# The minimum of a unit's scores, moved from behind the next unit's first eviction to in front of it

## What is computed

```python
q = _fq_sym(q, axis=-1)
k = _fq_sym(k, axis=-1)
v = _fq_sym(v, axis=2)
attn = jnp.einsum('bhqd,bhkd->bhqk', q, k)
attn = jax.nn.softmax(attn.astype(jnp.float32), axis=-1)
attn = _fq_unsigned(attn, axis=-1)
out = jnp.einsum('bhqk,bhkd->bhqd', attn, v)
```

## Time and profile before

| | us |
|---|---|
| median of three runs | 6005.62 (5996.2 to 6013.94) |
| the profiled execution, its own time | 5989.42 |
| its span (first to last instruction) | 5987.6 |
| VectorE busy in the span | 5458.4 (91%) |
| ScalarE busy | 4786.4 (80%) |
| GpSimd busy | 4741.8 (79%) |
| TensorE matmul busy | 4167.8 (70%) |
| first and last eviction of the cross attention (L918) start at | 344.9 and 5165.7 |

### The profile page before, as it was taken

The page is one execution under the profiler, slowest core; times in us unless marked ns, Lnnn a source line. Parts: engine busy times, 40 slices in busy tenths (PEclk is TensorE's granted clock), DMA queues, the critical chain, the costliest instruction groups (busy, mean ns, idle before and its releaser), DMA issues. The chain is left out here.

```text
span 5987.6 us, 141205 instructions
## 1 busy us (share of the span) xinstructions
PE 4167.8 (70%) x48324; PEld 2004.7 (33%) x49040; DVE 5458.4 (91%) x7655; ACT 4786.4 (80%) x6737; POOL 4741.8 (79%) x3414
## 2 busy tenths in 40 slices
PE   7656666666666666666666666666666666579898
PEld 3422222222222222222222222222222222346665
DVE  8889999999999999999999999999999999665444
ACT  5459999999899989989998899989999999646321
POOL 4558888888888888888888898888888888545351
PEclk9889999999999999999999999999999999889899
DMA  4167777777777777777777777777777777530243
GB/s 127 58 130 142 141 141 145 142 142 139 141 143 141 140 142 142 142 139 144 143 142 137 157 143 142 141 140 142 142 141 145 142 141 141 123 73 0 63 148 104
DMA packets 2282498, 783.42 MB, mean 131 GB/s; under 512 B 2189505, under 2 KB 2255908, under 8 KB 2276071
## 3 DMA queue, kind: packets, MB, share of 16 engines
q1 hardware_dynamic: 2239943, 604.79, 49.0%
q0 software_dynamic: 42272, 175.98, 15.6%
HBM read 187.41 MB, written 56.17 MB: 41 GB/s over the span
## 5 line engine op out<-in xcount | busy, mean ns | idle before, releaser
L918 DVE TENSOR_SCALAR_CACHE_REDUCE scores<-ring,step 128x2048 f32<-128x2048 f32 (+2 forms) x2560 | 4780.7, 1918 | 47.6 <-PE ring L845 35.5
L977 ACT ACTIVATE n_op<-scores,bias 128x2048 uint8<-128x2048 f32 x2048 | 4076.0, 1997 | 289.9 <-DVE m_rest L925 289.8
L793 POOL CAST nT<-pairs 128x2048 f16<-128x2048 uint8 x2048 | 3795.7, 1893 | 506.4 <-DMA pairs<-n_op 488.7
L845 PE MATMUL ring<-x_all,q_op 128*128 128x512 bf16 x7746 | 2149.8, 385 | 703.9 <-DVE scores L918 631.1
L845 PEld LDWEIGHTS ring<-x_all,q_op 128*128 128x128 bf16 x8192 | 683.2, 98 | 1856.2 <-DVE scores L918 1181.0
L842 PE MATMUL ring<-x_all,q_op 128*128 128x512 bf16 x1793 | 572.1, 389 | 778.6 <-DVE scores L918 747.6
L857 PE MATMUL pO<-nT,v_op 128*32 128x128 f16 x32768 | 659.7, 223 | 135.4 <-ACT att_g L995 109.4
L857 PEld LDWEIGHTS pO<-nT,v_op 128*32 128x32 f16 x32768 | 482.2, 98 | 585.1 <-issue 514.7
L842 PEld LDWEIGHTS ring<-x_all,q_op 128*128 128x128 bf16 x2048 | 116.8, 97 | 1001.6 <-DVE scores L918 983.6
L977 ACT ACTIVATION_READ_ACCUMULATOR n_op<-scores,bias 128x1 f32 x2048 | 395.1, 193 | 0.0
L1001 ACT COPY oT<-pO 128x512 f32<-128x512 f32 x128 | 75.0, 586 | 218.6 <-PE pO L857 218.6
(11 more groups left out here) (233 smaller groups left out, 3416.5 us busy)
## 6 DMA issues: line engine op xcount, KB each, us to landing
x_all<-keys_transposed POOLq DMA_DIRECT2D x128, 768.0 KB, 8.7
v_st<-value_integers POOLq DMA_DIRECT2D x128, 256.0 KB, 3.5
pairs<-n_op SPq DMA_TRANSPOSE x2048, 2.7
keys_transposed<-kT_s POOLq DMA_DIRECT2D x32, 384.0 KB, 3.3
xs<-expert_slots_in SPq DMA_DIRECT2D x78, 128.5 KB, 2.1
expert_slots_in<-zero_row SPq DMA_DIRECT2D x6, 1664.0 KB, 17.8
cT<-in_ctx_T SPq DMA_DIRECT2D x32, 256.0 KB, 2.6
z_all<-expert_outputs SPq DMA_DIRECT2D x4, 2048.0 KB, 11.7
```

The lines of the kernel that those rows point to most:

```text
L793: nc.gpsimd.tensor_copy(nT[par][:, j * EK:(j + 1) * EK, :].rearrange("p (a c) b -> p a c b", c=2), src).then_inc(s_un, 1)
L845: mm = nc.tensor.matmul(slot(t, j)[:, n * BANK:(n + 1) * BANK], q_op[b][:, t * P:(t + 1) * P], k_op[b][:, at + n * BANK:at + (n + 1) * BAN ...
L918: nc.vector.tensor_scalar(score[t % 2][:, at:at + width * BANK], slot(t, j)[:, 0:width * BANK], step[b][:, t:t + 1], None, ALU.mult, ALU.m ...
L977: nc.scalar.activation(n_op[par][:, j * EW:(j + 1) * EW], score[par][:, j * EW:(j + 1) * EW], ACT.Exp, bias=bias[par][:], scale=-1.0, accu ...
```

## The change

The two first entries of VectorE's list of steps change places.

```diff
-        DVE_STEPS = "D0 BIAS D1 D2 D3 INV D4".split()
+        DVE_STEPS = "BIAS D0 D1 D2 D3 INV D4".split()
```

## The result

| | before | after |
|---|---|---|
| time, median of 4 runs | 6000.91 us (5988.19 to 6013.94) | 6239.31 us (6237.09 to 6266.34) |
| profiled execution, own time | 5989.42 us | 6266.34 us |
| its span, mean granted clock of TensorE | 5987.6 us, 0.970 | 6263.8 us, 0.934 |

The change makes the kernel slower: 1.0407 times the time before, 95% interval 1.037 to 1.0445. That is 238 us between the medians, where 110 had been forecast, and outside the range.

What follows compares the result with a forecast made beforehand. The prediction took VectorE, busy 991 of 1000 us, as the bound. Its terms, 57 + 62 + 1 - 10 = 110 us, added to the median of 6005.62, gave 6116 us, with a range of 6050 to 6160.

Steps and rivals of the forecast that it cites:

- The minimum's own wait: Between D4's accumulator read and the minimum on VectorE: 0.112 us in each of 511 units, 57 us more.
- What is won: VectorE's waits for score buffers and TensorE's scores: earlier exponentials save 10 us, within bounds of nothing and 32.5 us.
- The register instructions: Between minimum and D0 in the loop: instructions preparing D0's waits no longer run ahead, 62 us more.
- Costed at nothing: ScalarE's, GpSimd's and TensorE's order.: The other engines' order: no cost, as they have 98, 114 and 321 us idle per 1000.
- if VectorE is found waiting for TensorE: Sign against the forecast: VectorE waiting for TensorE or ScalarE for more than the gaps at the seam between units.
- dearer seams: Rival at the seam between units: 0.35 us in place of 0.22, nothing won, 170 us more, 6176 us; chance 0.09.
- VectorE's busy share: Sign in the loop: falls from 99 to about 97%, with about 0.25 us more idle time or gap per unit.
- stay or grow: Sign on ScalarE: its total wait for the minimum, 289.8 us before, should not fall.
- Hidden register instructions: Rival between minimum and D0: VectorE's sequencer reads on past the waiting minimum, only the wait costs, 6054 us; chance 0.13.
- a free wait: Rival at the minimum behind D4: every start stays as before, time 6006 us; chance 0.05.
- a faster kernel: Rival at VectorE's waits for ring and score buffers: up to 32.5 us less, to 5973 us; chance 0.03.

Runs made afterwards that it cites:

- Experiment 6: The changed kernel with D0's two other waits moved ahead of D4, leaving one register instruction behind the minimum; 6131.31 us, ratio 1.0208 to the kernel before.
- experiment 1: The kernel before, in its old order, with D0 made to wait for D4's last column; 6161.09 us, ratio 1.026 to the kernel before.
- experiment 8: The changed kernel with an additional idle minimum behind D0, writing to a buffer nobody reads; 6205.2 us, ratio 1.0333 to the kernel before.
- Experiment 3: The changed kernel with two banks of the second part of even units computed twice on TensorE; 6117.07 us, ratio 1.0197 to the kernel before.
- experiment 2: The changed kernel with D0's waits taken in front of the minimum; 6170.34 us, ratio 1.0294 to the kernel before.

## Why the prediction was wrong

The sign was right, and the seam nearly so; a whole term was missing.

- **The minimum's own wait** (57 us). Right. The read starts and the minimum follows 0.118 us later (median of 512), against the 0.112 taken from the last unit, as in the fence above (2502.35 to 2502.48). That is 60 us; the distances add up to 70 because the minimum waited longer in 5 units (9.8 us, see "What is won"). "VectorE: DVE Perf Modes", The DRAIN you can't avoid, of the Trainium skill, says of a chain of copies that the semaphore after each costs nothing extra. The changed kernel's trace shows another case, a step that waits for the read just before it, and there the median is 0.118 us where it was 0.00.
- **The register instructions** (62 us). Right in kind, and a little too small. They start with the minimum, not ahead of it. The one of L694, then that of L917, at the seam whose minimum starts at 2502.48:

```profile
L694 DVEq FUSED_REGOPS  x1: 53/53/53, 2502.5 to 2502.5; - x1
...
L917 DVEq FUSED_REGOPS  x1: 57/57/57, 2502.6 to 2502.6; - x1
```

  D0 follows the minimum by 0.247 us (forecast 0.22), at the seam to another head by 0.333 (0.31), and outside the loop by 0.105 (0.09). These distances add up to 126 us, where the minimum had held D1 up by 40 before: 86 more, against a forecast of 62 + 1. The larger medians make 77 of it (288 x 0.169 + 96 x 0.255 + 127 x 0.027, each less the old 0.078); the rest are single longer waits. Experiment 6 leaves one of these instructions and D0 comes at 0.143. The Trainium skill's "Advanced Engine Details and Errata", Sequencer Loop, says that "Other engine instructions can be read & queued while ucode executes". Here the register instructions did not run ahead: at none of the loop's 384 seams does one of lines 694, 917 and 941 start before the minimum.
- The two terms together: 60 + 77 = 137 us by the medians, forecast 120. The seam as a whole grew by 124 only, because part of the waits that had stood in it is gone, as the next point says.
- **What is won** (10 us). Right in size, by luck. The forecast counted on the 8.5 us in front of ScalarE's buffers and on little of the 24 us for scores. It was the other way round: waits for scores in front of D0 fell from 11.5 us (30 waits) to 3.2 (9 waits), and those in front of D3 and D4 from 11.4 to 9.7, which is 10 us together. The 8.5 us of the earlier trace rows could not be won, for they are no waits for ScalarE. They are five turns of the hardware loop. At the first, the exponential that D0 needs had ended at 1556.23, but the register instruction of line 958, the loop's own, starts only at 1560.5, and D0 behind it (before, VectorE in order of time; then line 958's register instruction):

```profile
1558.94 0.09 DVE L918 DVE_READ_ACCUMULATOR scores<-ring,step 128x1 f32 x1
1560.77 1.82 DVE L918 TENSOR_SCALAR_CACHE_REDUCE scores<-ring,step 128x1536 f32<-128x1536 f32 x1 [1.74 <-ACT n_op L977]
...
L958 DVEq FUSED_REGOPS  x1: 118/118/118, 1560.5 to 1560.5; - x1
```

  The view names the last signal of the semaphore before D0, and not the one that D0 needed. With the change the minimum stands first behind the turn, and the five waits stand in front of it (VectorE's waits, 320 to 5450 us):

```profile
DVE m_rest L925 <- issue: 9.8, 5, 2.5
```

  Nor are the 84 waits of 14.1 us that the view puts down to ScalarE with the change waits for a buffer. All of them stand at the seam to another head, 0.17 us each between the minimum and D0, where the three register instructions lie, and the exponential needed had ended at least 2 us earlier.
- **"Costed at nothing: ScalarE's, GpSimd's and TensorE's order."** This is the step that failed. Its reason was TensorE's idle time, 321 us per 1000. But idle time in a view of 1000 us says nothing of where the idle time lies. TensorE's pause at the seam ends with D0 and so is made of VectorE's time; what the seam gained, the pause gained, too (0.36 and 0.35 us). Behind the pauses of before (median 1.47 us) the clock was full, behind those of the change it fell in 144 of 255 cases, and M2's six matmuls, which before had been done within D1's 1.74 us, then kept D2 waiting for 1 us: 153 us in all, the term that the sum lacked. The forecast's text had named this as a sign of being wrong ("if VectorE is found waiting for TensorE"), but gave it no rival and no price. The stretch of the earlier trace rows had a granted clock of 0.98, so the trace of before showed that the clock does fall in this kernel; what it would have taken is to ask which pauses of TensorE the change makes longer, and what a part of scores costs at half clock against the eviction beside it.
- **The range.** Its upper end took in dearer seams alone. A rival "TensorE late behind the seam" with half of the even units at 1 us each, 255 / 2 x 1 = 128 us, would have reached 6244 us; that it would be about half is known only afterwards.
- **What would show it.** VectorE's busy share fell to 95.3% instead of 97, by the new waits. ScalarE's wait for the minimum fell from 289.8 to 181.2 us, where "stay or grow" was forecast. ScalarE's idle time is only placed elsewhere: its waits for the value product grew from 218.6 to 608.6 us. Before:

```profile
L1001 ACT COPY oT<-pO 128x512 f32<-128x512 f32 x128 | 75.0, 586 | 218.6 <-PE pO L857 218.6
```

- **The rivals.** Hidden register instructions, a free wait and a faster kernel are all excluded by the seam's rows. The fourth, dearer seams, fails too: the seams cost 124 us more, and not its 170. (Of the three instructions in its row, one is a semaphore wait.)

What stays open: why 144 of 255 long pauses end in a fall with the change, 69 and 66 with an additional 0.08 us of VectorE's work per unit, and 38 in experiment 1, at pauses of nearly the same length. The length of the pause alone does not decide: with the change it is 1.82 us in the median with a fall and without one, and in the kernel before 26 of the 255 pauses were of 1.7 to 1.8 us, too, and none ended in a fall. The units' rhythm may have part in it, since experiment 8 alters little else against the change; what decides wasn't shown, nor whether the early exponentials do. Experiment 3 both shortens the pause and adds work ahead of it, and which of these keeps the clock up was not separated either. No variant beat the kernel before.

## What to carry to other kernels

On the engine that sets the pace, put independent work between a result and the step that waits for it: a small step right behind its producer cost 0.12 us here, and what prepares the next step's waits cannot run ahead of it and came on top, 0.25 us from the minimum to the next eviction. Before you count another engine as idle enough, look at where it pauses, whether the change lengthens that pause, and whether the work behind it still fits if the clock falls. Where such a loss has come about, a little redundant work ahead of the pause, or less of it behind, took nearly all of the waiting away.

## What the runs showed of the hardware that was not expected

- A TensorE pause of 1.8 to 1.9 us between two parts of scores was followed by half clock in up to 144 of 255 cases; in the kernel before, with a median of 1.47 us at the same place, in none of 255. With the change, the 144 falls and the 144 waits of over 0.3 us before D2 are those of the same units.
- More work made the kernel faster: experiment 8 is the changed kernel with 512 more minima on its busiest engine (40 us), and took 6205 us instead of 6239 (1.0333 times the kernel before, instead of 1.0407).
- Which instruction carries a wait has a price: with another step's waits placed ahead of it, the same minimum started 0.21 us after the read it waits for instead of 0.12 (experiment 2).
- A loop's turn on VectorE: between the last eviction's read in one pass and the first step of the next lay 1.6 to 2.6 us with the change, against 0.12 us at other seams. The table of waits had put the same time, before the change, down to ScalarE.
